# Products of the identity ahead of TensorE's waits, and the stores of x2 moved to SyncE, in a fused decoder layer

## The chip, the cores and the metric

The kernel runs on one NeuronCore of one Trainium2 chip. The metric is the device time of one execution in microseconds (us). The engines are TensorE (PE, with its weight loads as PEld), VectorE (DVE), ScalarE (ACT), GpSimd (POOL) and SyncE (SP, which only issues transfers).

## The reference

One layer over x of shape (32, 256, 256), all in float32, cut to what matters:

```python
x = layernorm(x + mamba(x, ...))               # conv, silu, softplus, scan over 16 states
x = layernorm(x + cross_attention(x, ctx))     # 16 heads of 16, 256 queries x 256 keys
x = layernorm(x + expert_ffn(x))               # 8 experts, D_FF = 704; tokens split by position
```

In cross_attention each head makes `scores = q @ k.T / sqrt(16)`, a softmax, and `attn @ v`; the 16 heads are joined and multiplied by `w_o`. In expert_ffn expert e works on positions 32e to 32e+31 of every one of the 32 batches (`h = silu(x @ w1[e]) * (x @ w3[e]); out = h @ w2[e]`), so the experts start when the last batch has left the second layernorm.

## The kernel before, in words

There are two programs, one after the other on the same core: `mixers` (mamba and attention, batch by batch) and `experts`. Within `mixers` every engine has its own list of steps. `run_steps` (its code stands below) sorts them by a number: a step with offset o runs for batch b at position 16*b + o, and steps at one position in the order of the list. So up to six batches are in flight at once, and one engine works in strict program order: a step that waits holds up all that stands behind it.

**The attention of a batch.** The queries and keys are split into high and low parts, stored to DRAM (`store_parts`), and loaded back stacked by SP (`load_stack(gr)`, lines 430 and 432: nine transfers for four heads; it waits until the previous batch's `scores_T` has read these heads). PE makes `scores(hd)` (tile s_ps, or dA_ps0 at the end), DVE takes the row maximum (`row_max`, L863), PE transposes the maxima of four heads (`max_transpose`, L1100), ACT and DVE split them (L716, L869), and ACT stores and reloads them as two more rows of q_st (L726, L735: max_rows_dram). Then PE makes the scores again, transposed (`scores_T`, tile st_ps or dA_ps1), ACT takes the exponential (L679, probs), and PE multiplies by v (`pv(gr)`, f_ps<-probs,v). ACT evacuates (L690, oT), PE transposes back (`head_transpose(gr)`, L1143), DVE normalises (L883, L888, tile on). PE transposes `on` (L1060), ACT evacuates (L696), PE makes `attn_out` (a_ps<-w_o,x1T), DVE adds the residual and takes moments (L838 to L847), ACT normalises (L631 to L642, `norm(1, ...)`), which completes x2 of the batch in x_tok. It is then stored to DRAM as rows (`store_x2`, L671, four transfers, x_rows<-x_tok, issued by ACT), and transposed by PE (L1060, a_ps<-ident,x_tok), evacuated by ACT (L705; of the last batch first its first columns, L703) and stored as columns (`store_x2T`, L463, issued by SP).

**The drain.** After the scans of batch 31 (POOL has then nothing more to do, and DVE only its part of the attention) PE, ACT and DVE finish the attention of batches 29, 30 and 31. Meanwhile SP loads weights of the first expert (L184, L190), then, in `load_tokens` and `load_columns`, the tokens of the first expert. `load_columns` waits for the stored columns of batch 30 (L175, 96 KB). At the end of `mixers` all engines meet (L200) and `experts` begins on PE with `gate_up` (L1376: g_ps and u_ps), which waits for these columns.

**Precision.** The operands of the scores are float32r (rounded), read in one record per product; a product of ordinary float32 operands shows as two MATMUL records in the trace, and a PE transpose as one. The count x8 on a row of the trace with float32 operands is thus four products.

PE's transposes and products share three PSUM banks (`bank_a`, `bank_f`, `bank_y`), and `wait_read` waits until a bank's last content has been read.

Of the kernel before, what the change touches and what calls it, by code (L numbers as in the profile page):

```python
# [14 lines left out]
P = 128  # L15
B, L, D = 32, 256, 256
# [5 lines left out]
TT = L // P  # L22
H, DK = 16, 16
HG = 4
NG = H // HG
# [5 lines left out]
EC = L // E  # L31
# [17 lines left out]
NX = 4  # L49
# [26 lines left out]
O_ONT = 78  # L76
O_OF = 80
O_N2 = 82
# [117 lines left out]
def mixers(nc, io, x2_dram, scratch, shared):  # L196
# [3 lines left out]
    with ExitStack() as ctx:  # L200
# [144 lines left out]
        def _(sp):  # L345
# [112 lines left out]

            def store_x2T(b):

                dst = shared.x2T_dram.rearrange("k e p t -> p (k e) t")[:, :, EC * b.c:EC * (b.c + 1)]
                wait_all(sp, (s_x2T, 1, b, 1))
                sp.dma_start(dst, x2T[:].rearrange("p k (e t) -> p (k e) t", t=EC)).then_inc(s_x2T_st, 16)  # L463
# [16 lines left out]
                *[(O_LD + HG * gr - 2, load_stack(gr)) for gr in range(NG)],  # L480
                (O_X2T + 3, load_columns),
# [58 lines left out]
        def _(act):  # L540
# [124 lines left out]
            def store_x2(b):  # L665

                rows = x2_dram.rearrange("(a e n r) d -> n e r a d", a=TT, e=P // EC, r=EC)
                rows = rows[bass.ds(b.c, 1)].rearrange("n e r a d -> (n e) r a d")
                wait_all(act, (s_x2, TT, b, TT))
                for q in range(X2_DMAS):  # L670
                    act.dma_start(rows[q], xt[EC * q:EC * (q + 1), b.c % NX]).then_inc(s_x2_st[b.par], 16)  # L671

# [57 lines left out]
            def max_load(gr):  # L730
# [14 lines left out]
                (O_N2 + 3, store_x2),  # L745
# [170 lines left out]
        def _(pe):  # L916
# [8 lines left out]

            pe.wait_ge(s_zero, 1)
# [121 lines left out]

            def x_of(b):
                return xt[:, b.c % NX]  # L1050
# [28 lines left out]
            def scores(hd):  # L1079

                def piece(b):
                    pe.wait_ge(s_stack[hd // HG], b.value(STACK_DMAS * 16, STACK_DMAS * 16))
                    n = b.value(H, hd)
                    if n:
                        pe.wait_ge(s_max, n - 1 if n > LATE_S + 1 else n)
                    if n == LATE_S + 1:
                        pe.wait_ge(s_hC_v, len(HC_DVE) * B)
                        for half in range(2):
                            pe.wait_ge(s_scan[half], NU * B)
                    out = scores_bank(n)  # L1090
                    for tt in range(TT):
                        i = mm(out[:, tt], q_st[:, hd, tt * P:(tt + 1) * P], k_st[:, hd], True, True)
                    i.then_inc(s_s_mm, 1)
                return piece

            def max_transpose(gr):
                def piece(b):
                    pe.wait_ge(s_max, b.value(H, HG * gr + HG))
# [7 lines left out]
            def scores_T(hd):  # L1106

                def piece(b):
                    pe.wait_ge(s_m_row, b.value(NG * 16, 16 * (hd // HG) + 16))
# [7 lines left out]
                    out = scores_T_bank(n)  # L1117
                    for kt in range(TT):
                        i = mm(out[:, kt], k_st[:, hd, kt * P:(kt + 1) * P], q_st[:, hd], True, True)
# [3 lines left out]
            def pv(gr):  # L1123

                def piece(b):
                    pe.wait_ge(s_exp, b.value(H, HG * gr + HG))
# [11 lines left out]
            def head_transpose(gr):  # L1138
                def piece(b):
                    pe.wait_ge(s_oT, b.value(NG, gr + 1))  # L1140
# [8 lines left out]
            def attn_out(tt):  # L1149
                def piece(b):  # L1150
                    pe.wait_ge(s_onT, b.value(1, 1))
# [22 lines left out]
                *[(O_K, k_proj(m)) for m in range(KD)],  # L1174
                (O_ONT - 2, transpose(lambda b: on, s_on, NG, s_onT_mm, s_onT, bank_a, a_ps)),
                *[(O_Q, q_proj(m)) for m in range(KD)],
                (O_X2T, transpose(x_of, s_x2, TT, s_x2T_mm, s_x2T, bank_a, a_ps)),
                *[(O_ON + HG * gr, head_transpose(gr)) for gr in range(NG)],
# [318 lines left out]
```

## Time and profile before

| | |
|---|---|
| time, median of 3 runs | 2745.58 us (2741.46 to 2746.72) |
| the profiled execution | 2741.8 us; its span 2740.0 us |
| PE busy | 2429.5 us (89%) |
| DVE busy | 2123.5 us (77%) |
| ACT busy | 1821.1 us (66%) |
| POOL busy | 2073.6 us (76%) |
| mean granted TensorE clock | 0.952 |

The span runs from the first to the last instruction. Busy shares are means over the stages: POOL works in `mixers` only and is idle from about 2159 us on; `experts` starts at 2257.47 us and is work of PE without a gap nearly to the end. The granted clock is given as a share of 2.4 GHz: 1.00 is 2.4 GHz, 0.50 is 1.2 GHz, and numbers between are means over a stretch that has both.

### The profile page before, as it was taken

The numbers are of one execution on the slowest core, as the hardware profiler recorded it, in microseconds if no ns is written. First come the engines' busy times: TensorE is split into PE (matmuls) and PEld (weight loads), VectorE is DVE, ScalarE is ACT, GpSimd is POOL, SyncE is SP. The second block draws the span as 40 slices with busy tenths as digits, with TensorE's granted clock in tenths as the row PEclk, the third lists the DMA queues.
The fourth block names the chain that finished last, engine by engine and source line by source line (L and its number), as shares of the span: only waits on it lengthen the run. The fifth ranks groups of instructions, "written<-read, shape, count | busy, mean of one in ns | idle before, by whom it ended". The sixth has DMA issues, their size and how long they took to land. (4 is left out here: it accounts for less than half of the span.)

```text
span 2740.0 us, 49530 instructions
## 1 busy us (share of the span) xinstructions
PE 2429.5 (89%) x14854; PEld 1667.0 (61%) x14854; DVE 2123.5 (77%) x3232; ACT 1821.1 (66%) x3972; POOL 2073.6 (76%) x999
## 2 busy tenths in 40 slices
PE   6678898989898898889999989988997879999997
PEld 5456666666666666666666666666665545555554
DVE  3788999999999999999999999999999722222333
ACT  3667888888888888888888887888887531111111
POOL 5999999999999999999999999999999400000000
PEclk9888999999999999999999999999998869999999
DMA  5355666666666666666666666666665342432221
GB/s 154 112 152 147 168 168 161 160 167 170 175 161 168 171 171 163 163 165 167 165 165 176 160 177 162 171 163 160 160 160 156 101 118 65 119 120 80 80 80 31
DMA packets 270168, 399.66 MB, mean 146 GB/s; under 512 B 115441, under 2 KB 190449, under 8 KB 265810
## 3 DMA queue, kind: packets, MB, share of 16 engines
q1 hardware_dynamic: 254546, 384.95, 52.9%
q10 hardware_dynamic: 15360, 11.55, 1.6%
q8 instruction: 124, 2.03, 0.3%
q14 instruction: 138, 1.13, 0.2%
HBM read 300.89 MB, written 94.37 MB: 144 GB/s over the span
## 5 line engine op out<-in xcount | busy, mean ns | idle before, releaser
L519 POOL TENSOR_TENSOR arena<-arena 128x1024 f32<-128x1024 f32 x512 | 1207.6, 2364 | 33.6 <-DMA arena<-w_dram 33.3
L623 ACT ACTIVATE dA_ps<-arena,a_neg 128x256 f32<-128x256 f32 x2048 | 880.1, 465 | 256.3 <-DVE arena L800 125.7
L800 DVE TENSOR_TENSOR_SCAN arena<-dA_ps,arena 128x512 f32<-128x512 f32 x672 | 802.7, 1207 | 75.5 <-ACT dA_ps L623 52.2
L529 POOL TENSOR_TENSOR arena<-arena 128x1024 f32<-128x1024 f32 (+1 forms) x416 | 808.4, 1943 | 18.0 <-DVE arena L800 15.0
L800 DVE TENSOR_TENSOR_SCAN dA_ps<-dA_ps,arena 128x512 f32<-128x512 f32 x352 | 415.7, 1204 | 3.8 <-POOL arena L519 3.4
L920 PE MATMUL a_ps<-xT,w_conv 128*128 128x256 f32 x1536 | 367.3, 389 | 0.0
L863 DVE TENSOR_REDUCE mx<-s_ps 128x2 f32<-128x512 f32 x497 | 333.4, 671 | 18.6 <-PE s_ps L920 18.6
L920 PEld LDWEIGHTS a_ps<-xT,w_conv 128*128 128x128 f32 x1536 | 286.5, 193 | 53.9 <-issue 16.3
L679 ACT ACTIVATE probs<-st_ps 128x512 f32<-128x512 f32 x493 | 285.2, 578 | 27.6 <-PE st_ps L920 25.4
L920 PE MATMUL s_ps<-k_st,q_st 96*128 96x256 f32 x994 | 262.2, 346 | 38.8 <-DVE mx L863 29.3
L920 PE MATMUL y_ps<-arena,sel 128*32 128x256 f32 x4096 | 258.5, 395 | 37.5 <-POOL arena L529 33.9
L920 PE MATMUL st_ps<-q_st,k_st 96*128 96x256 f32 x986 | 220.3, 306 | 35.3 <-ACT probs L679 29.6
L813 DVE TENSOR_TENSOR arena<-dA_ps,arena 128x512 f32<-128x512 f32 x352 | 230.7, 676 | 4.4
L920 PEld LDWEIGHTS s_ps<-k_st,q_st 96*128 96x128 f32 x994 | 167.8, 197 | 85.6 <-issue 55.3
L920 PEld LDWEIGHTS st_ps<-q_st,k_st 96*128 96x128 f32 x986 | 156.0, 196 | 96.1 <-issue 85.1
L1305 DVE TENSOR_TENSOR hT<-silu,u_ps 128x512 f32<-128x512 f32 x80 | 54.9, 686 | 193.8 <-PE u_ps L1376 161.0
L920 PEld LDWEIGHTS y_ps<-arena,sel 128*32 128x32 f32 x4096 | 126.4, 113 | 128.0 <-POOL arena L529 34.1
L1278 ACT ACTIVATE silu<-g_ps 128x512 f32<-128x512 f32 (+1 forms) x96 | 56.4, 596 | 210.0 <-PE g_ps L1376 209.9
L1376 PE MATMUL g_ps<-arena 128*128 128x512 f32 x384 | 181.7, 599 | 2.7 <-PEq L200 2.7
L920 PE MATMUL a_ps<-bias 2*128 2x512 f32 (+2 forms) x192 | 93.0, 485 | 98.5 <-DVE parts L853 39.9
L920 PE MATMUL f_ps<-probs,v 128*32 128x256 f32 x2048 | 156.0, 428 | 0.8 <-ACT probs L679 0.7
L1376 PE MATMUL u_ps<-arena 128*128 128x512 f32 x320 | 150.5, 592 | 0.0
(117 smaller groups left out, 3275.4 us busy)
## 6 DMA issues: line engine op xcount, KB each, us to landing
arena<-delta_dram SPq DMA_DIRECT2D x512, 128.0 KB, 2.9
arena<-w_dram SPq DMA_DIRECT2D x512, 128.0 KB, 3.3
arena<-bc_dram SPq DMA_DIRECT2D x128, 256.0 KB, 4.5
q_st<-q_parts_dram SPq DMA_DIRECT2D x512, 64.0 KB
k_st<-k_parts_dram SPq DMA_DIRECT2D x512, 64.0 KB
w_dram<-u SPq DMA_DIRECT2D x32, 512.0 KB, 3.1
delta_dram<-delta SPq DMA_DIRECT2D x32, 512.0 KB, 3.9
k_parts_dram<-parts SPq DMA_DIRECT2D x32, 512.0 KB, 4.2
```

What stands on the lines that cost most here:

```text
L519: pool.tensor_tensor(dBu[:, n % NB], w_r[:, n // RP % 2, t % RP].unsqueeze(1).to_broadcast([P, QS, L]), bc_r[:, b.par, 0], ALU.mult).then_ ...
L529: pool.tensor_tensor(h[:, n % NH, states], h[:, n % NH, states], bc_r[:, b.par, 1, states], ALU.mult).then_inc(s_hC, 1)
L623: last = nc.scalar.activation(dA[n % NDA][:, q], delta_r[:, n // (2 * RP) % 2, t % RP], ACT.Exp, scale=a_neg[:, t, 2 * half + q:2 * half + ...
L679: nc.scalar.activation(probs[:, n % NPROB], scores_T_bank(n), ACT.Exp, scale=float(DK) ** -0.5).then_inc(s_exp, 1)
L800: nc.vector.tensor_tensor_scan(dst, decays, dBu[:, n % NB, 2 * half:2 * half + 2].rearrange("p q t -> p (q t)"), 0.0, ALU.mult, ALU.add).t ...
L813: nc.vector.tensor_tensor(h[:, n % NH, 2 * half:2 * half + 2], state[:], bc_r[:, b.par, 1, 2 * half:2 * half + 2], ALU.mult).then_inc(s_hC ...
L863: nc.vector.tensor_reduce(mx[:, hd], scores_bank(b.value(H, hd)), AX.X, ALU.max).then_inc(s_max, 1)
L920: return nc.tensor.matmul(out, lhsT, rhs, start=first, stop=last)
L1278: nc.scalar.activation(dst, g_ps[i % 2][first:last], ACT.Silu).then_inc(f_silu, 1)
L1305: nc.vector.tensor_tensor(hT[first:last, i // 2, HALF * (i % 2):HALF * (i % 2 + 1)], silu[first:last, i % 2], ups[first:last], ALU.mult).t ...
L1376: ins = nc.tensor.matmul(ps[i % 2][:], w13[:, b.par, k, col:col + P], x2T[:, b.par, k, cols], start=(k == 0), stop=(k == KD - 1))
```

## The change

Two things change. First, PE is given products of the identity with itself (`drain_products`, 128x128 float32, into a bank that nobody reads then) in front of the waits of the last batch: 11 before the scores of head 0, 4 before each of the first two transposes of maxima, 6, 6 and 12 before the transposed scores of heads 4, 8 and 12, 5 before `pv` of the last two groups, 4, 22, 4 and 5 before the four `head_transpose`, 4 before the transposes of `on`, 5 before `attn_out`, 34 before the transposes of x2 and 16 behind them; and 11 before the second `head_transpose` of batch 30. These are 158 products. In `scores` and `scores_T` the wait for the loaded rows moves behind them. Second, `store_x2` goes from ACT's list (offset O_N2 + 3) to SP's (O_N2 + 4), for all 32 batches.

```diff
@@ -456,6 +456,14 @@
+            def store_x2(b):
+
+                rows = x2_dram.rearrange("(a e n r) d -> n e r a d", a=TT, e=P // EC, r=EC)
+                rows = rows[bass.ds(b.c, 1)].rearrange("n e r a d -> (n e) r a d")
+                wait_all(sp, (s_x2, TT, b, TT))
+                for q in range(X2_DMAS):
+                    sp.dma_start(rows[q], xt[EC * q:EC * (q + 1), b.c % NX]).then_inc(s_x2_st[b.par], 16)
+
@@ -478,6 +486,7 @@
                 *[(O_LD + HG * gr - 2, load_stack(gr)) for gr in range(NG)],
+                (O_N2 + 4, store_x2),
                 (O_X2T + 3, load_columns),
                 (O_X2T + 3, store_x2T),
@@ -662,14 +671,6 @@
-            def store_x2(b):
...
@@ -742,7 +743,6 @@
-                (O_N2 + 3, store_x2),
@@ -923,6 +923,15 @@
+            def drain_products(b, count, out=None):
+                if b.c < B - 1:
+                    return
+                if out is None:
+                    bank_y.wait_read(pe)
+                    out = y_ps[:, 0:P]
+                for _ in range(count):
+                    mm(out, ident[:], ident[:], True, True)
+
@@ -1046,6 +1055,11 @@
+            def idle(count):
+                def piece(b):
+                    drain_products(b, count)
+                return piece
+
@@ -1079,7 +1093,6 @@
             def scores(hd):
                 def piece(b):
-                    pe.wait_ge(s_stack[hd // HG], b.value(STACK_DMAS * 16, STACK_DMAS * 16))
...
                     out = scores_bank(n)
+                    drain_products(b, {0: 11}.get(hd, 0), out[:, 0, 0:P])
+                    pe.wait_ge(s_stack[hd // HG], b.value(STACK_DMAS * 16, STACK_DMAS * 16))
@@ -1095,6 +1110,7 @@
             def max_transpose(gr):
                 def piece(b):
+                    drain_products(b, 4 if gr < 2 else 0)
                     pe.wait_ge(s_max, b.value(H, HG * gr + HG))
@@ -1106,7 +1122,6 @@
             def scores_T(hd):
-                    pe.wait_ge(s_m_row, b.value(NG * 16, 16 * (hd // HG) + 16))
...
                     out = scores_T_bank(n)
+                    drain_products(b, {4: 6, 8: 6, 12: 12}.get(hd, 0), out[:, 0, 0:P])
+                    pe.wait_ge(s_m_row, b.value(NG * 16, 16 * (hd // HG) + 16))
@@ -1123,6 +1140,7 @@
             def pv(gr):
+                    drain_products(b, 5 if gr >= NG - 2 else 0)
@@ -1137,6 +1155,9 @@
             def head_transpose(gr):
+                    drain_products(b, (4, 22, 4, 5)[gr])
+                    if gr == 1 and b.c == B - 2:
+                        drain_products(b.ahead(1), 11)
@@ -1148,6 +1169,7 @@
             def attn_out(tt):
+                    drain_products(b, 5 if tt == 0 else 0)
@@ -1172,9 +1194,12 @@
+                (O_ONT - 2, idle(4)),
                 (O_ONT - 2, transpose(lambda b: on, s_on, NG, s_onT_mm, s_onT, bank_a, a_ps)),
                 *[(O_Q, q_proj(m)) for m in range(KD)],
+                (O_X2T, idle(34)),
                 (O_X2T, transpose(x_of, s_x2, TT, s_x2T_mm, s_x2T, bank_a, a_ps)),
+                (O_X2T, idle(16)),
```

On PE, at the end of `mixers` (from the last `head_transpose` of batch 31 on, then the first products of `experts`), before:

```order
L1143 MATMUL f_ps<-ident,oT 128x128 x2
L1060 MATMUL a_ps<-ident,on 128x128 x4
L1060 MATMUL a_ps<-ident,x_tok 128x128 x4
L920 MATMUL a_ps<-bias 128x512
L920 MATMUL a_ps<-w_o,x1T 128x256 x4
L1060 MATMUL a_ps<-ident,x_tok 128x128 x4
L200 UNCONDITIONAL_BRANCH
L1354 UNCONDITIONAL_BRANCH
L1376 MATMUL g_ps<-arena 128x512 x2
```

And in the changed kernel, the same place (line numbers have moved: 1143 is 1164, 1060 is 1074, 1376 is 1401):

```order
L1164 MATMUL f_ps<-ident,oT 128x128 x2
L920 MATMUL y_ps<-ident 128x128 x4
L1074 MATMUL a_ps<-ident,on 128x128 x4
L1074 MATMUL a_ps<-ident,x_tok 128x128 x4
L920 MATMUL y_ps<-ident 128x128 x5
L920 MATMUL a_ps<-bias 128x512
L920 MATMUL a_ps<-w_o,x1T 128x256 x4
L920 MATMUL y_ps<-ident 128x128 x34
L1074 MATMUL a_ps<-ident,x_tok 128x128 x4
L920 MATMUL y_ps<-ident 128x128 x16
L200 UNCONDITIONAL_BRANCH
```

The order of the real products is the same; 59 identity products stand between them, 34 of them directly in front of the transposes of x2 and 16 in front of the meeting of the engines.

On PE, earlier in the drain (batch 31 alone: `scores_T` of heads 8 to 12, `pv(1)`, `head_transpose(1)`), in the changed kernel:

```order
L920 MATMUL st_ps<-ident 128x128 x6
L920 MATMUL st_ps<-q_st,k_st 128x256 x2
L920 MATMUL f_ps<-probs,v 32x256 x8
L920 MATMUL dA_ps1<-q_st,k_st 128x256 x2
L920 MATMUL st_ps<-q_st,k_st 128x256 x2
L920 MATMUL y_ps<-ident 128x128 x22
L1164 MATMUL f_ps<-ident,oT 128x128 x2
L920 MATMUL dA_ps1<-q_st,k_st 128x256 x2
L920 MATMUL st_ps<-ident 128x128 x12
L920 MATMUL st_ps<-q_st,k_st 128x256 x2
```

Before, the same rows stand there without the three that read only `ident`.

On SP, the end of `mixers`, from the weights of the first expert to the columns of batch 31, before:

```order
L184 DMA arena<-in_w 128x2x704
L463 DMA x_columns<-x2T_batch 128x16x32
L175 DMA arena<-x_columns 128x2x896
L170 DMA arena<-x_rows 128x7x256
L463 DMA x_columns<-x2T_batch 128x16x32
L175 DMA arena<-x_columns 128x2x96
L463 DMA x_columns<-x2T_batch 128x16x32
```

And in the changed kernel:

```order
L465 DMA x_rows<-x_tok 32x2x256 x4
L184 DMA arena<-in_w 128x2x704
L471 DMA x_columns<-x2T_batch 128x16x32
L465 DMA x_rows<-x_tok 32x2x256 x4
L175 DMA arena<-x_columns 128x2x896
L170 DMA arena<-x_rows 128x7x256
L471 DMA x_columns<-x2T_batch 128x16x32
L465 DMA x_rows<-x_tok 32x2x256 x4
L175 DMA arena<-x_columns 128x2x96
L471 DMA x_columns<-x2T_batch 128x16x32
```

The three rows of L465 are the stores of batches 29, 30 and 31. That of 29 stands behind `load_stack(2)` and ahead of `load_stack(3)` of batch 31 (not shown), that of 30 ahead of the tokens of the first expert, and that of 31 ahead of the 96 KB of columns on which `gate_up` waits.

## Rows read from the trace of the kernel before

**Rows 1.** The page: 40 slices of the span, and one of the costliest groups.

```profile
POOL 5999999999999999999999999999999400000000
PEclk9888999999999999999999999999998869999999
...
L519 POOL TENSOR_TENSOR arena<-arena 128x1024 f32<-128x1024 f32 x512 | 1207.6, 2364 | 33.6 <-DMA arena<-w_dram 33.3
```

**Rows 2.** Windows of the drain: stretch, its length, busy (records) by engine, PEclk.

```profile
2200.50:2214.40 13.90, 13.53 (x74) 10.12 (x75) 6.79 (x14) 5.95 (x12) 0.00 (x0) 0.50 0.49 138
2229.20:2257.50 28.30, 16.22 (x70) 9.21 (x70) 3.24 (x13) 8.53 (x20) 0.00 (x0) 0.52 0.17 38
```

**Rows 3.** Timeline of PE in the drain: start, length, work, count [idle before].

```profile
2194.36 0.51 PE L920 MATMUL s_ps<-k_st,q_st 96*128 96x256 f32 x2 [1.59 <-DMA q_st<-k_st]
...
2198.84 0.41 PE L1143 MATMUL f_ps<-ident,oT 128*128 128x128 f32 x2 [1.58 <-ACT oT L690]
...
2207.39 0.77 PE L920 MATMUL s_ps<-k_st,q_st 96*128 96x256 f32 x2
...
2214.49 0.78 PE L920 MATMUL s_ps<-k_st,q_st 96*128 96x256 f32 x2
...
2229.19 0.41 PE L1143 MATMUL f_ps<-ident,oT 128*128 128x128 f32 x2 [3.07 <-ACT oT L690]
...
2231.77 0.80 PE L920 MATMUL st_ps<-q_st,k_st 96*128 96x256 f32 x2 [1.63 <-DMA q_st<-max_rows_dram]
...
2245.66 3.78 PE L920 MATMUL a_ps<-w_o,x1T 128*128 128x256 f32 x8
2253.69 1.12 PE L1060 MATMUL a_ps<-ident,x_tok 128*128 128x128 f32 x4 [4.25 <-ACT x_tok L642]
2257.47 3.75 PE L1376 MATMUL g_ps<-arena 128*128 128x512 f32 x4 [2.67 <-PEq L200]
```

**Rows 4.** Timeline of PE, the spacing of small products at the full clock.

```profile
2155.73 1.99 PE L920 MATMUL a_ps<-w_o,x1T 128*128 128x256 f32 x8
...
2179.70 0.40 PE L920 MATMUL s_ps<-k_st,q_st 96*128 96x256 f32 x2
2179.94 0.40 PE L920 MATMUL st_ps<-q_st,k_st 96*128 96x256 f32 x2
...
2188.55 0.60 PE L1060 MATMUL a_ps<-ident,x_tok 128*128 128x128 f32 x4
```

**Rows 5.** The same timeline at the very start of the kernel.

```profile
1.18 9.04 PE L920 MATMUL s_ps<-g 128*128 128x256 f32 x32 [1.18 <-DVE g L765]
```

**Rows 6.** The chain that ended last, a later group of gate_up.

```profile
2262.99 1.72 PE g_ps L1376 x4
```

**Rows 7.** Timeline of all engines, the end of batch 31.

```profile
2248.06 0.36 SPq L175 DMA_DIRECT2D arena<-x_columns  x1
...
2252.56 1.08 ACT L642 ACTIVATE x_tok<-x_tok,shift,rstd 128x256 f32<-128x256 f32 x2
2253.66 1.76 ACTq L671 DMA_DIRECT2D x_rows<-x_tok  x4
```

**Rows 8.** Timeline of SP, the stacked loads of batch 31.

```profile
2192.00 0.59 SPq L432 DMA_DIRECT2D q_st<-k_st  x1
...
2199.88 0.30 SPq L430 DMA_DIRECT2D q_st<-q_parts_dram  x1
...
2203.52 0.59 SPq L432 DMA_DIRECT2D q_st<-k_st  x1
```

**Rows 9.** Timeline of SP and ACT in a batch of the steady stage.

```profile
1238.95 1.08 ACT L642 ACTIVATE x_tok<-x_tok,shift,rstd 128x256 f32<-128x256 f32 x2
...
1252.27 0.60 SPq L432 DMA_DIRECT2D q_st<-k_st  x1
...
1261.77 1.71 SPq L395 DMA_DIRECT2D arena<-delta_dram  x4
```

**Rows 10.** DMA issues near the end of mixers: size, median us to landing.

```profile
arena<-x_columns SPq DMA_DIRECT2D x1, 96.0 KB, 2.4
```

More of the change, by code:

```diff
@@ L663, in bc_store @@
                 act.dma_start(bc_dram[b.par], xp[RANK:RANK + 2 * NS]).then_inc(s_bc_st, 16)
-            def store_x2(b):
[L667 to L671, printed above, removed]
             def softmax_exp(hd):
```

## The prediction

> **What bounds the kernel now.** I read the page first. POOL shows 9 in nearly every slice of `mixers`, so up to about 2159 us the elementwise products of the scan set the pace; its one large wait is for a load of w, 33.3 us in all [rows 1]. From 2257.47 us on the last chain is PE without a break: the experts [rows 3, 6]. Between lies the drain, some 100 us, in which PE is busy but hands over to ACT, DVE and transfers again and again. The PEclk line has its one 6 there [rows 1]. The windows show why: 0.50, the lower level of 1.2 GHz, from 2200.50 to 2214.40, and 0.52 from 2229.20 to the end of `mixers` [rows 2]. What the engine did before each fall stands in its timeline: it had waited 1.59 and 1.58 us shortly before 2200, and 3.07 us just before 2229.19 [rows 3]. The price of the low clock is seen best on equal work: the eight records of `attn_out` take 1.99 us at 2155.73 [rows 4] and 3.78 us at 2245.66 [rows 3]; the first four of `gate_up` take 3.75 us [rows 3], the same form later 1.72 [rows 6].
>
> So there is something to win. What is at stake is the start of `gate_up`, 2257.47, and the pace of its first records; behind it nothing changes.
>
> **What a product costs.** This is the number on which all hangs, and the trace has no float32 product of 128 columns. An ordinary float32 product is two records; with 256 columns, eight records take 1.99 us, about 0.21 each after the first. The stream of 128 columns would be half of that, 0.107 a record, 0.213 us a product. But each record also loads 128 weight columns. The nearest rows with loads of that width and a stream of 0.107 us are the scores (two records of 256 float32r columns): pairs start at 2179.70 and 2179.94, so 0.24 us for two records [rows 4]. I take 0.24 us a product at the full clock, with 0.213 as the near bound. The far bound is the transpose, also 128x128 float32 but one record: four in 0.60 us, (0.60 - 0.27)/3 = 0.11 us each, where 0.27 is the tail of the last one [rows 4]. At the low clock all of these double, as `attn_out` does. 158 products are 38 us of PE at 0.24 (34 at 0.213, 17 at 0.11).
>
> The waits of PE that they are put into are shorter than that. 11 products are 2.64 us for a wait of 1.59; the other 11 stand in one of 1.58; 22 are 5.3 us for 3.07; 12 are 2.9 for 1.63; 34 are 8.2 for 4.25; 16 are 3.8 for 2.67 [rows 3]. At 0.11 each run fits its wait (1.2, 1.2, 2.4, 1.3, 3.7, 1.8). The wait of 4.25 is the clearest: it is the residual, moments and layernorm on DVE and ACT, from the end of `attn_out` at 2249.44 to the end of L642 at 2253.64 [rows 3, 7], and no clock of PE shortens or lengthens it.
>
> The Trainium skill (FP8 and Floating Point Precision, section TensorE Precision Notes) says that a true float32 product takes four passes through the array. That agrees with the records of 256 columns above (1.99 us for four products, less the tail, is near 4 x 256 columns at 2.4 GHz each), and by it alone a product of 128 columns is 0.213 us, the near bound; the sum would then be the -2.4 us below.
>
> **The drain replayed.** I walk through PE's order with 0.24 us for a product, the full clock for everything, and the measured durations for what ACT, DVE and the transfers do.
> - Scores of head 0 of batch 31: 11 products from 2192.6, so 2195.3, not 2194.36. The second run of 11 starts at 2198.2 and ends at 2200.85, where `head_transpose` had started at 2198.84: 2.0 us late.
> - The scores of heads 8 to 11 come 6.1 us after the `scores_T` that frees their rows: 4.2 us in which SP issues nine transfers (2199.88 to 2204.11) and 1.8 us of landing (the last issue of the first stack ends at 2192.59, its reader starts at 2194.36) [rows 3, 8]. That `scores_T` ends at 2201.8 in the replay, 2.0 us late, so the reader starts at 2207.9, against 2207.4 before: there it did not wait for its load, and the low clock had used up the slack.
> - Between the stacks of heads 8 to 11 and 12 to 15 SP now issues the four stores of batch 29, 1.8 us [rows 7], so the last stack is issued at 2208.0 to 2212.2 and read at 2214.0. It was read at 2214.5 [rows 3]: SP's own store eats what the clock would give here.
> - From there the scores, `pv` and the transposes run at the full clock, but 6 + 4 + 6 products (3.8 us) go in: `scores_T` of head 8 at 2223.5. Then 22 products: `head_transpose(1)` at 2230.4 (2229.19 before), 1.2 us late. Then 12: `scores_T` of head 12 at 2233.8 (2231.77), 2.0 us late.
> - 5, 4, 5 and 5 more, each in a wait of some 0.6 us, against half the time for 16 records of `pv` twice: the last `head_transpose` at 2241.3. The transposes and `attn_out`, at the full clock and with 4 and 5 products, end at 2247.5 against 2249.44: 1.9 us early.
> - 34 products: the transposes of x2 start at 2255.6 instead of 2253.69, although x2 is ready at 2251.7. 16 products and 0.7 us for the engines to meet: `gate_up` at 2260.6, 3.1 us late.
> - `gate_up` then starts at the full clock: 3.75 becomes 1.72, -2.0 us [rows 3, 6].
>
> Sum: +3.1 - 2.0 = +1.1 us. The same walk at 0.213 us puts the same places at 2195.0, 2207.4, 2213.5, 2229.1, 2232.2, 2245.4, 2252.5 and 2257.1: -0.4 - 2.0 = -2.4 us. I forecast the middle of these two, -0.7 us. At most places the ends of the two walks differ by less than the counts suggest, because part of each run still lies in a wait.
>
> **The stores on SP.** In the steady stage each batch adds four issues, 1.8 us, to SP, behind a stacked load and ahead of the next load of delta. SP idles there from 1252.87 to 1261.77, 8.9 us [rows 9], waiting for its turn with that buffer; x2 is ready 12 us before, at 1240.03, so the stores neither wait nor delay the load. If the cover were gone it would be 1.8 us for each of 32 batches, 58 us, but some 7 us of it remain. ACT loses 1.8 us of issue a batch, which it did beside its activations; POOL is the bound [rows 1], so I put this at nothing. At the very end it frees ACT: L703 waited until the issue at 2253.66 was over, 1.76 us long [rows 7], about 0.7 us behind the transposes. That is hidden behind PE's 16 products. In its place `load_columns` moves behind the four stores of batch 31: 96 KB that were asked for at 2248.06 are now asked for 1.8 us after the layernorm and land 0.4 + 2.4 us later [rows 7, 10], 4.6 us after it: 2256.3 in my replay, hidden as long as the products hold PE to 2260. If PE were earlier, this becomes the wait that starts the experts.
>
> **Rivals.**
> - *A product costs what a transpose does (0.11 us).* For it: same shape, same operand. Against it: no ordinary float32 product in the trace shows as one record. The overruns vanish; the replay then has 2212.0 for head 12 (-2.5, SP's stack), 2224.3 for `head_transpose(1)` (-4.9), 2226.0 for head 12 transposed (-5.8), the end of `attn_out` at 2237.4 (-12.0), x2 ready at 2241.6, and `gate_up` at 2246.2, held by the 96 KB: -11.3 - 2.0 = -13.3 us, 2732.3 us.
> - *The low clock stays, slower than before.* The windows say that the scores and `pv` alone do not raise it: PE was busy 13.53 of 13.90 us at 0.50 [rows 2]. At the start of the kernel 32 records in 9.04 us, where 32 x 0.213 are 6.8, say that some 10 dense records ran at half speed first [rows 5]. If the clock falls at about 2205 again, where only 4 products stand in 7 us, then 6 + 4 + 6 + the first 9 of the 22 run at 0.48: 25 x 0.24 = +6.0 us, and what the clock gave between is gone as well: +1.1 + 6.0 + 1 = +8 us, 2753.7 us. This decides from about 20 products at the low clock on.
> - *The stores held on SP delay a load in the steady stage.* Only where SP's idle time of 8.9 us shrinks under 1.8; no batch that I looked at does. Its price from one such batch in four would be 8 x 1.8 = 14 us.
>
> **How the numbers follow.** The replay with its two prices, 0.5; the cheap product, 0.3, since it alone makes every run of products fit its wait; the low clock, 0.15; the stores, 0.05. The profiled execution before took 2741.8 us, 3.8 under the median of 2745.58; I add the difference of -0.7 to the median: 2744.9. The likeliest case alone holds 2741 to 2749 (prices of 0.213 to 0.26, and some microseconds of the runs' own spread, 2741.46 to 2746.72). For eight in ten the range goes to the cheap product below, 2732, and most of the way to the low clock above, 2751. A measurement of this kernel can tell 0.2%, 5.5 us. Faster by more: the cheap product, and a little of the replay's low side, 0.33. Slower by more: low clock, stores, 0.17. Within: 0.5.
>
> **What would show it.** In the profile after: the mean spacing of the 34 products (8.2 us in all; 7.3 or 3.7 by the bounds); a transposition of x2 that starts at once behind them while x2 has been ready for 3 us or more; PEclk near 1.00 from 2192 to 2262, with 2205 to 2214 as the doubtful part; `gate_up` in 1.72 us from its first group; SP's stores between the last two stacked loads. A product at 0.11 us makes the forecast wrong, and then `gate_up` should wait for the 96 KB of columns.

## The result, and the profile after

The changed kernel takes 2750.52 us (median of 20 runs, 2744.6 to 2756.96), the kernel before, run beside it, 2743.14 us (20 runs, 2737.86 to 2747.37). The ratio is 1.0025, interval 1.0016 to 1.0034: some 7 us slower. The forecast was no change, with -0.7 us. The execution whose profile is shown took 2745.45 us, 5.1 us under its kernel's median, so the profiled pair shows only part of the loss.

The page after, against [rows 1]; 40 slices, then two of the costliest groups (L528 is L519 of before, L538 was L529):

```profile
POOL 5999999999999999999999999999999400000000
PEclk8798999999999999999999999999998899999999
...
L528 POOL TENSOR_TENSOR arena<-arena 128x1024 f32<-128x1024 f32 x512 | 1209.9, 2369 | 27.3 <-DMA arena<-w_dram 26.8
L538 POOL TENSOR_TENSOR arena<-arena 128x1024 f32<-128x1024 f32 (+1 forms) x416 | 811.0, 1950 | 26.3 <-DVE arena L800 24.0
```

The 6 in PEclk is gone, so the products did what they are there for. But POOL's second group now waits 26.3 us. Its first group waits less than in [rows 1], 27.3 us against 33.6, so the two together wait 53.6 us against 51.6. The second group's row of before:

```profile
L529 POOL TENSOR_TENSOR arena<-arena 128x1024 f32<-128x1024 f32 (+1 forms) x416 | 808.4, 1943 | 18.0 <-DVE arena L800 15.0
```

The windows of the drain answer to [rows 2], moved by 2.0 us at the first and 4.1 to 5.4 us at the second:

```profile
2202.50:2216.40 13.90, 11.59 (x101) 8.84 (x101) 7.43 (x17) 7.22 (x16) 0.00 (x0) 1.00 0.42 109
2233.30:2262.90 29.60, 28.42 (x252) 26.04 (x250) 3.25 (x13) 7.72 (x18) 0.00 (x0) 1.00 0.34 92
```

The clock is 1.00 where it was 0.50 and 0.52. The timeline of PE answers to [rows 3]:

```profile
2194.89 0.27 PE L1116 MATMUL y_ps<-ident,mx 128*8 128x128 f32 x1
2194.99 2.62 PE L920 MATMUL s_ps<-ident 128*128 128x128 f32 x22
2197.37 0.48 PE L920 MATMUL s_ps<-k_st,q_st 96*128 96x256 f32 x2
...
2209.57 0.47 PE L920 MATMUL s_ps<-k_st,q_st 96*128 96x256 f32 x2 [0.50 <-DMA q_st<-k_st]
...
2216.19 0.47 PE L920 MATMUL s_ps<-k_st,q_st 96*128 96x256 f32 x2 [1.33 <-DMA q_st<-k_st]
...
2228.46 5.08 PE L920 MATMUL y_ps<-ident 128*128 128x128 f32 x44
2233.38 0.38 PE L1164 MATMUL f_ps<-ident,oT 128*128 128x128 f32 x2
...
2248.90 1.99 PE L920 MATMUL a_ps<-w_o,x1T 128*128 128x256 f32 x8
2250.73 7.75 PE L920 MATMUL y_ps<-ident 128*128 128x128 f32 x68
2258.32 0.60 PE L1074 MATMUL a_ps<-ident,x_tok 128*128 128x128 f32 x4
2258.76 3.74 PE L920 MATMUL y_ps<-ident 128*128 128x128 f32 x32
2262.95 1.95 PE L1401 MATMUL g_ps<-arena 128*128 128x512 f32 x4 [0.45 <-PEq L200]
```

x68 are the records of 34 products. Less the tail of the last one, a product is (7.75 - 0.27)/34 = 0.220 us, between the forecast's two prices. x2 was ready at 2255.09 (end of L651, once L642), and its transposes begin 3.2 us later, when the products are through; with half the products (an experiment below) they follow x2 in 0.5 us.

### Two stretches in which the time is counted

I measure every kernel below in the same two stretches.

- *Steady stage*: from the second MEMSET of delta on POOL to the 32nd; there is one a batch.
- *Drain*: from the transposition of maxima directly ahead of the scores of head 0 of batch 31 to the end of the first group of `gate_up`. (That transposition is the last of batch 30; some expectations below call it `max_transpose(1)` of batch 31, and mean the same row.)

The first two marks, on POOL's timeline, before:

```profile
92.59 0.13 POOL L510 MEMSET delta<- 128x16 f32 x1
2074.10 0.12 POOL L510 MEMSET delta<- 128x16 f32 x1
```

and after:

```profile
92.57 0.13 POOL L519 MEMSET delta<- 128x16 f32 x1
2077.35 0.13 POOL L519 MEMSET delta<- 128x16 f32 x1
```

So the steady stage is 1981.5 us before and 1984.8 after, +3.3. The drain is 68.7 before (2192.50 to 2257.47 + 3.75) and 70.0 after (2194.89 to 2262.95 + 1.95): +1.3, close to the forecast's +1.1. The forecast's sum for the drain held; most of what was measured lies where it expected nothing. One profile of each can't carry that alone, so the experiments had to.

Between the two stretches lie another 118.4 us before and 117.5 after. Over all profiles below this piece is 118.5 us in the mean with the old order of two waits and 117.8 with the new one (single values 115.8 to 120.4), so it doesn't hide a loss.

### The profile page after: what moved, and what is told of

It is laid out like the page before. It is cut to its first block and busy times, and to the rows that moved or that the text cites. A ratio compares the mean times of both kernels' runs of the same rounds, so it can differ in the third digit from the quotient of the medians.

```text
span 2743.6 us, 50161 instructions
## 1 busy us (share of the span) xinstructions
PE 2453.4 (89%) x15170; PEld 1692.6 (62%) x15170; DVE 2122.6 (77%) x3232; ACT 1821.7 (66%) x3972; POOL 2074.9 (76%) x999
## 5 line engine op out<-in xcount | busy, mean ns | idle before, releaser
L528 POOL TENSOR_TENSOR arena<-arena 128x1024 f32<-128x1024 f32 x512 | 1209.9, 2369 | 27.3 <-DMA arena<-w_dram 26.8
L800 DVE TENSOR_TENSOR_SCAN arena<-dA_ps,arena 128x512 f32<-128x512 f32 x672 | 802.4, 1207 | 70.8 <-ACT dA_ps L632 52.4
L538 POOL TENSOR_TENSOR arena<-arena 128x1024 f32<-128x1024 f32 (+1 forms) x416 | 811.0, 1950 | 26.3 <-DVE arena L800 24.0
L800 DVE TENSOR_TENSOR_SCAN dA_ps<-dA_ps,arena 128x512 f32<-128x512 f32 x352 | 415.7, 1204 | 5.3 <-POOL arena L528 3.4
L920 PE MATMUL y_ps<-arena,sel 128*32 128x256 f32 x4096 | 258.8, 395 | 36.4 <-POOL arena L538 34.5
```

What stands on the lines that cost most here:

```text
L528: pool.tensor_tensor(dBu[:, n % NB], w_r[:, n // RP % 2, t % RP].unsqueeze(1).to_broadcast([P, QS, L]), bc_r[:, b.par, 0], ALU.mult).then_ ...
L538: pool.tensor_tensor(h[:, n % NH, states], h[:, n % NH, states], bc_r[:, b.par, 1, states], ALU.mult).then_inc(s_hC, 1)
L800: nc.vector.tensor_tensor_scan(dst, decays, dBu[:, n % NB, 2 * half:2 * half + 2].rearrange("p q t -> p (q t)"), 0.0, ALU.mult, ALU.add).t ...
L920: return nc.tensor.matmul(out, lhsT, rhs, start=first, stop=last)
```

## The experiments

All medians are of 5 to 12 runs of the variant against 29 to 35 of before. First the four that take the change apart.

**Stores alone.** No products; the stores on SyncE and the moved waits stay.

```diff
 def drain_products(b, count, out=None):
-    if b.c < B - 1:
-        return
+    return
```

> Stores of x2 on SyncE, no identity product at all. Theory A (the whole loss is the products that overrun their waits): within 2 us of the kernel before, at most +1 us since the 96 KB of columns are now asked for behind the four stores. Theory B (the products cost only some 1 to 4 us as in the profiled pair, and the stores on SyncE cost the rest in the steady stage): +4 to +6 us over the kernel before.

Measured: 2743.12 us, ratio 1.0008 (0.9994 to 1.0021), some 2 us, between the two theories and too near to both for the interval to tell. The drain is 65.2 us, 3.5 less than before, which neither theory had.

**Products alone.** `store_x2`, with ScalarE as the issuer again, is back in its list.

```diff
-                (O_N2 + 4, store_x2),          # SyncE
+                (O_N2 + 3, store_x2),          # ScalarE
```

> All 158 products, stores of x2 on ScalarE as before. Theory A: +6 to +8 us over the kernel before, as the changed kernel. Theory B: +1 to +2 us.

Measured: 2754.18 us, ratio 1.0040 (1.0026 to 1.0054), the slowest of all: 11 us over before, more than either theory had (+6 to +8, +1 to +2). Its drain is 74.5 us. Windows of it, with the clock ahead of the last two columns:

```profile
2205.00:2216.00 11.00, 9.68 (x86) 8.29 (x84) 5.91 (x13) 6.19 (x16) 0.00 (x0) 1.00 0.47 126
2216.00:2226.00 10.00, 8.36 (x51) 6.61 (x51) 3.67 (x9) 3.52 (x7) 0.00 (x0) 0.66 0.79 244
```

and its timeline of PE there:

```profile
2216.92 0.77 PE L920 MATMUL st_ps<-q_st,k_st 96*128 96x256 f32 x2 [1.52 <-DMA q_st<-max_rows_dram]
...
2226.91 0.50 PE L920 MATMUL st_ps<-q_st,k_st 96*128 96x256 f32 x2 [1.63 <-DMA q_st<-max_rows_dram]
```

Here the clock falls once more: it is 0.50 from 2217 to 2223, behind a wait for the rows of maxima, which ScalarE stores and reloads. Less the 7.1 us by which this drain began later than before's, that is 2210 to 2216, in and just behind the stretch that the rival of the low clock called doubtful (2205 to 2214). This kernel differs from the changed one only in who issues the stores, so with them on ScalarE the products did not hold the clock; the evidence is one profile of each.

**Half of every count** (76 products), and **half of the last two runs only** (34 to 17, 16 to 8).

```diff
-                (O_X2T, idle(34)),
+                (O_X2T, idle(17)),
...
-                (O_X2T, idle(16)),
+                (O_X2T, idle(8)),
```

> Both parts of the change, but about half of every count of products (76 in place of 158: 17 and 8 at the end), so that at 0.226 us a product each run fits its wait. Theory A: the overruns vanish and the clock stays high, gate_up starts 11 us or more before that of the changed kernel, so some 5 us under the kernel before. Theory B: the same gain in the drain, less 5 us lost in the steady stage, so also 11 us under the changed kernel. If the clock falls in the drain instead, it is no faster than the kernel before.

> The change with only the last two runs halved, 17 and 8 in place of 34 and 16. Both theories: the transposes of x2 start when x2 is ready, 3.2 us earlier, and gate_up then waits for the 96 KB of columns, so 3 to 3.5 us under the changed kernel.

Measured: half of all 2739.93 us, 0.9991 (0.9980 to 1.0003), drain 61.5; half of the tail 2744.47 us, 1.0008 (0.9996 to 1.0020), drain 67.9. The last transposes now follow x2 within 0.5 us. The clock of the kernel with half of all is 1.00 from 2192 to 2254. It does not last to the end: `gate_up` waits for the 96 KB and then starts at the low clock, 3.68 us for its first group where the changed kernel has 1.95:

```profile
2257.84 3.68 PE L1401 MATMUL g_ps<-arena 128*128 128x512 f32 x4 [1.94 <-DMA arena<-x_columns]
```

So too with half of the tail (3.36 us, behind a wait of 1.97). There `gate_up` starts 3.5 us earlier in the drain than in the changed kernel, as expected, and loses 1.4 of it again to the clock. Halving the tail thus takes 2.1 us off the drain, halving the rest another 6.4, so the runs of products ahead of the tail cost more than the tail. The gain in time of half of all, some 2 us, is what its theory B leaves, not the 5 us of theory A.

These four fell into a pattern: each took 3 to 6 us more than its drain gave. What they all share with the changed kernel, and not with before, is the order of two waits in all 32 batches.

**The waits alone; before once more; the whole change with the old order of the waits in batches 0 to 30.** The edit of the last:

```diff
 def scores(hd):
     def piece(b):
+        if b.c < B - 1:
+            pe.wait_ge(s_stack[hd // HG], ...)
...
         drain_products(b, {0: 11}.get(hd, 0), out[:, 0, 0:P])
-        pe.wait_ge(s_stack[hd // HG], ...)
+        if b.c == B - 1:
+            pe.wait_ge(s_stack[hd // HG], ...)
```

and the same in `scores_T` with s_m_row.

> No products, stores of x2 on ScalarE as before; of the change only this is left: in scores and scores_T the wait for the loaded rows stands behind the wait for the free bank, in all 32 batches. Before this run, the five changed kernels sit 3 to 6 us above what their profiled drains (from max_transpose(1) of batch 31 to the first group of gate_up) would give against the profiled execution of before. Theory A, the swapped waits cost something small in each batch: ratio 1.001 to 1.002, 3 to 6 us above before. Rival B, the offset comes from the one profiled execution of before, whose drain or start was not typical: ratio 1.000 within 0.0008. Rival C, it comes from the stores or the products: also 1.000 here.

> The kernel before, unchanged, as if it were a variant: ratio 1.000, its own interval shows what the comparison can tell. Its second profile is what is wanted. Rival B: max_transpose(1) of batch 31 lies 2 us or more after the 2192.5 us of the first profile, as in all five changed kernels (2194.2 to 2201.6), or the stretch from it to the first group of gate_up, the group included, is 3 us or more off the 68.7 us of the first profile. Theory A or C: it lies at 2192.5 within 1.5 us and the stretch is 68.7 within 1.5 us.

> The changed kernel with all its 158 products and the stores on SyncE, but in batches 0 to 30 the wait for the loaded rows stands ahead of the wait for the bank again, as before; only in batch 31 it stands behind the products. Theory A: the offset goes, ratio about 1.0005 (the +1.3 us of the drain alone), against 1.0025 of the changed kernel. Rivals B and C: as the changed kernel, 1.002 to 1.003.

Measured: the waits alone 2747.68 us, 1.0023 (1.0011 to 1.0035); before again 2744.03 us, 1.0004 (0.9993 to 1.0016), steady stage 1984.6, drain 68.4; the whole change with the old order 2741.51 us, 1.0001 (0.9992 to 1.0010). Two lines of code that look like tidying, and nothing else, cost as much as the whole change did, within the intervals. Taking them back takes the loss back, with all 158 products still in. That is theory A, a little above its 1.001 to 1.002. Of rival B one sign came true: in the second profile of before the first mark of the drain lies at 2198.36, 5.9 us later than in the first, whose `mixers` were thus on the short side. But the drain agrees (68.4 against 68.7), and before again takes the same time as before.

The waits of POOL between 250 and 2160 us (us in total, times, longest) tell the two orders apart. Before:

```profile
POOL arena L519 <- DMA arena<-w_dram: 17.4, 20, 2.2
POOL arena L529 <- DVE arena L800: 15.0, 21, 1.9
```

The changed kernel:

```profile
POOL arena L538 <- DVE arena L800: 23.3, 25, 1.9
POOL arena L528 <- DMA arena<-w_dram: 11.9, 16, 1.7
```

The whole change with the old order:

```profile
POOL arena L528 <- DMA arena<-w_dram: 22.3, 29, 1.8
POOL arena L538 <- DVE arena L800: 13.8, 19, 1.9
```

In the new order POOL, the bound of this stage, waits 8 to 10 us longer for VectorE's scans and 5 to 10 us less for its loads of w. In these three profiles the one nearly makes up for the other. The cost shows over all 17 profiles: POOL is busy for 1934.7 to 1936.3 us of the steady stage in each of them, and all its waits between 250 and 2160 us add up to 45 us in the mean with the old order in `scores_T` (42.9 to 47.0) and to 51 with the new one (45.9 to 54.8). The changed kernel's profile has the 45.9, the lowest of its group.

**Columns first.** With half of the products `gate_up` waited 1.94 us for the 96 KB. Here their load is issued ahead of the stores of batch 31.

```diff
+                (O_N2 + 4, load_columns),
                 (O_N2 + 4, store_x2),
-                (O_X2T + 3, load_columns),
```

> Half of the products at each place (76 in all), stores of x2 on SyncE, and the last load of columns (96 KB) is issued ahead of the four stores of batch 31. With half the products (ratio 0.9991) the first group of gate_up waited 1.94 us for these columns, behind the stores. If that wait is SyncE's order of issue, it goes, gate_up follows the transposes of x2 and the 8 products at once, and the time is 1.9 us lower: ratio 0.9984, the stretch from max_transpose(1) to the end of the first group 59.6 us against 61.5. Rival: the columns are late for another reason (the layernorm frees nothing earlier, or the landing of 2.4 us), then 61.5 stays and the ratio is 0.9991.

Measured: 2737.90 us, 0.9987 (0.9977 to 0.9997); the drain 58.6 us, 2.9 less than with half the products alone. The wait was SyncE's order of issue, and the rival falls. Only 1.2 us of the 2.9 are the earlier start; the other 1.7 are the first group, which runs at the full clock again (1.96 us against 3.68), and the expectation did not have that. Its timeline at the end:

```profile
2244.51 0.36 SPq L175 DMA_DIRECT2D arena<-x_columns  x1
2246.91 1.08 ACT L651 ACTIVATE x_tok<-x_tok,shift,rstd 128x256 f32<-128x256 f32 x2
2248.01 1.75 SPq L465 DMA_DIRECT2D x_rows<-x_tok  x4
2248.04 0.66 PE L1074 MATMUL a_ps<-ident,x_tok 128*128 128x128 f32 x4 [0.46 <-ACT x_tok L651]
...
2251.09 1.96 PE L1401 MATMUL g_ps<-arena 128*128 128x512 f32 x4 [0.60 <-PEq L200]
```

The columns are asked for 3.5 us ahead of the stores, and `gate_up` waits only for the meeting of the engines.

**All of it together, and the parts of the swap.** The version that the runs pointed to (half of the products, columns first, old order of the waits); the swap of the waits in `scores` alone and in `scores_T` alone, on the kernel before; and the stores on SyncE alone with the old order.

```diff
 def scores_T(hd):
     def piece(b):
-        pe.wait_ge(s_m_row, b.value(NG * 16, 16 * (hd // HG) + 16))
...
         out = scores_T_bank(n)
+        pe.wait_ge(s_m_row, b.value(NG * 16, 16 * (hd // HG) + 16))
```

> What the runs so far point to: half of the products (76), stores of x2 on SyncE, the last columns loaded ahead of the stores of batch 31, and in batches 0 to 30 the waits in the order of before. If the pieces add up, with the swapped waits that kernel is 0.9987, and the swap alone costs 0.0023: ratio 0.9965 to 0.997, 2733 to 2734 us, and GpSimd's last MEMSET of delta lies 1981 to 1985 us behind its second, as in the three profiles with the old order, not 1984.5 to 1992.5. Rival: the swap costs nothing once the stores are on SyncE, ratio 0.9987.

> The kernel before with the waits swapped in scores alone (stack behind bank), without products or other changes. The swap of both costs 1.0023 (5 to 6 us). If it is the first wait of scores that costs, the ratio is 1.002 and GpSimd waits 22 to 31 us for scans of VectorE between 250 and 2160 us (14 to 15 with the old order); if it is that of scores_T, 1.000 and 14 to 15 us.

> The kernel before with the waits swapped in scores_T alone (rows of maxima behind bank). If it is the wait of scores_T that costs, the ratio is 1.002 and GpSimd waits 22 to 31 us for VectorE; if that of scores, 1.000 and 14 to 15 us. If each gives half, 1.001 both times, the cost lies in many small shifts.

> Of the change only the stores of x2 on SyncE, for all 32 batches, the waits in the order of before in batches 0 to 30, no products. The same with swapped waits was 1.0008 with a drain (max_transpose(1) of batch 31 to the end of the first group of gate_up) of 65.2 us against 68.7. If the prediction was right that the stores cost nothing in the steady stage, only the drain is left: -3 us, ratio 0.9988. If they cost there, 1.000 or above.

Measured: all together 2733.75 us, 0.9966 (0.9949 to 0.9983), some 9 us faster than before, as expected (its steady stage, 1985.9 us, is 1 us outside the range given); `scores` swapped 2744.40, 1.0004 (0.9987 to 1.0020); `scores_T` swapped 2745.47, 1.0010 (0.9996 to 1.0024); stores alone with the old order 2736.86, 0.9977 (0.9962 to 0.9992), so they cost nothing in the steady stage. In time neither half of the swap stands apart from no change, and neither reached the 1.002 named for it. In the trace they differ: POOL waits 25.8 us for L800 with `scores_T` swapped, within the 22 to 31 named, and 18.6 with `scores` swapped, between the two ranges named. With the stores alone, `gate_up` shows the wait that the forecast named for the case that PE is early:

```profile
2252.53 1.75 SPq L465 DMA_DIRECT2D x_rows<-x_tok  x4
...
2254.32 0.44 SPq L175 DMA_DIRECT2D arena<-x_columns  x1
2256.97 3.78 PE L1406 MATMUL g_ps<-arena 128*128 128x512 f32 x4 [3.31 <-DMA arena<-x_columns]
```

**A second wait in `scores_T`, and the whole change with one of the two orders old.**

```diff
 # the kernel before, scores_T: the wait ahead stays
         out = scores_T_bank(n)
+        pe.wait_ge(s_m_row, b.value(NG * 16, 16 * (hd // HG) + 16))
```

> The kernel before with one more wait in scores_T: the rows of maxima are waited for ahead of the bank, as before, and once more behind it, where they have long arrived. If what costs is that a wait already met stands between the wait for ScalarE's exponential and the product (theory A in its narrow form), the traces of the swapped kernels come back: GpSimd waits 22 to 31 us for VectorE between 250 and 2160 us, ScalarE's evacuation of v waits 15 to 19 us, the ratio is about 1.001. Rival: what costs is that the wait for the rows is taken late, then 12 to 16 us and 25 to 30 us, and 1.000.

> The changed kernel, with the old order of the waits in scores_T alone (batches 0 to 30). The swap alone in scores_T left the marks in the trace, that in scores hardly. So most of the offset should go: ratio 1.0005 to 1.001 (the changed kernel 1.0025, with both old 1.0001). Rival: both matter, about 1.0013.

> The changed kernel, with the old order of the waits in scores alone (batches 0 to 30), scores_T swapped as in the change. If scores_T carries the cost, the ratio stays at 1.002 to 1.0025 and GpSimd waits 22 to 31 us for VectorE; if scores carries it, 1.0005.

Measured: the second wait 2746.15 us, 1.0012 (1.0002 to 1.0023), POOL waits 31.4 us for L800; the whole change with `scores_T` in the old order 2745.66, 1.0010 (0.9997 to 1.0023), 14.9 us; with `scores` in the old order 2748.44, 1.0021 (1.0010 to 1.0033), 24.7 us. The waits of POOL follow `scores_T`. The times point the same way, as both expectations had it, though these two intervals overlap.

What the second wait tells depends on where the waits stand in the program as built. A product carries one wait itself, and others stand in a semaphore instruction ahead of it. The order of the built program, before:

```
L920 MATMUL st_ps<-q_st,k_st 128x256 [waits probs_ready,max_rows_loaded]
```

and, the same with `scores_T` swapped, with the second wait and in the changed kernel:

```
L920 MATMUL st_ps<-q_st,k_st 128x256 [waits max_rows_loaded,probs_ready]
```

```profile
L1112 PEldq EVENT_SEMAPHORE  x510: 51/51/51, 213.5 to 2235.8; - x170
L1117 PEldq EVENT_SEMAPHORE  x511: 51/51/51, 213.3 to 2241.4; - x171
L1118 PEldq EVENT_SEMAPHORE  x512: 51/51/2599, 209.3 to 2248.4; - x171
```

L1112 is the wait for the exponential, L1117 that for the rows of maxima. So the wait written first stays on the product (on its weight load, in the trace), and the one written later goes ahead of it. Before, the product carries the wait for the rows, and the wait for the exponential stands ahead of it. With `scores_T` swapped, and in the changed kernel, it is the other way round: the move behind the bank in the source is a move ahead in the built program. With the second wait (L1118) the extra instruction waits for both, and the product once more for the rows. That is a third form and no repetition of the swap.

All three forms differ in how soon PE starts when the exponential ends its wait. From the end of the exponential to the product it is 0.145 us before (28 places of the trace, 0.144 to 0.146), 0.053 with the swap and in the changed kernel (23 places each, 0.052 to 0.053), and 0.10 with the second wait (25 places, 0.098 to 0.100). Both quicker forms have the longer waits of POOL for L800 (25.8 and 31.4 us, against 15.0), and the ratios 1.0010 and 1.0012. ScalarE's wait for the product of v, of which the expectation speaks, divides the profiles too: 25.8 to 29.6 us in the seven with the old order in `scores_T`, 14.8 to 18.7 in the ten others, 17.1 with the second wait. So the marks that the expectation named for its theory came. The theory itself falls all the same: it blames a wait already met that stands between the wait for the exponential and the product, and that is just what before has, without the marks, and what the swapped kernels do not have.

The Trainium skill (Perfetto Trace Analysis, section Identifying Dependency Chains) says that an instruction which waits on several engines may get an extra semaphore instruction ahead of it for the rest. The traces agree: some 510 such instructions for the 512 heads of `scores_T` (16 in each of 32 batches). Which of the two waits stays on the product is decided by the order in the source.

### All variants in one table

Expected sum: 5.4 us where `scores_T` waits in the new order, plus the drain less 68.5 (the mean of the six without products and with the stores on ScalarE). Measured is (ratio - 1) x 2743; the intervals of these ratios are 2.5 to 4.7 us to either side.

| kernel | POOL <- L800 | steady stage | drain | sum | measured |
|---|---|---|---|---|---|
| before; again | 15.0; 13.9 | 1981.5; 1984.6 | 68.7; 68.4 | 0 | 0; +1.1 |
| `scores` swapped | 18.6 | 1983.0 | 70.1 | +1.6 | +1.1 |
| `scores_T` swapped; second wait | 25.8; 31.4 | 1985.4; 1993.6 | 68.3; 68.0 | +5.2; +4.9 | +2.7; +3.3 |
| both swapped | 30.8 | 1989.5 | 67.7 | +4.6 | +6.3 |
| stores, old order | 12.2 | 1981.4 | 65.1 | -3.4 | -6.3 |
| stores, new order | 28.7 | 1984.6 | 65.2 | +2.1 | +2.2 |
| products, new order | 25.5 | 1991.2 | 74.5 | +11.4 | +11.0 |
| **the change** | 23.3 | 1984.8 | 70.0 | +6.9 | +6.9 |
| the change, old order | 13.8 | 1982.0 | 69.9 | +1.4 | +0.3 |
| the change, `scores_T` old; `scores` old | 14.9; 24.7 | 1983.3; 1987.7 | 70.3; 69.9 | +1.8; +6.8 | +2.7; +5.8 |
| half tail | 28.2 | 1992.5 | 67.9 | +4.8 | +2.2 |
| half of all | 22.7 | 1991.1 | 61.5 | -1.6 | -2.5 |
| half, columns first | 28.3 | 1984.7 | 58.6 | -4.5 | -3.6 |
| half, columns first, old order | 14.3 | 1985.9 | 58.7 | -9.8 | -9.3 |

The seven profiles with the old order in `scores_T` have a steady stage of 1983.1 us in the mean (1981.4 to 1985.9), the ten with the new one 1988.5 (1984.6 to 1993.6); this is where 5.4 comes from. The second wait counts with the new order. The sums miss the measured by up to 2.9 us, so the table shows that the parts fit together, and not what each is worth to a microsecond. A single profile wanders by several microseconds there, so that no single pair would have shown it; the waits of POOL separate the two groups without overlap (12.2 to 18.6 and 22.7 to 31.4).

## Why the prediction was wrong

- **The step that failed is one that it did not take.** In the part on the change it costs the products, the clock and the stores, but puts no price on the moved waits in `scores` and `scores_T`, though the text on the change names them and they act in all 32 batches. They are worth some 6 us (1.0023 alone, 6.3 us; 1.0025 against 1.0001 in the whole change, 6.6 us). It looked for the change in the drain only, because there the products are. The text on the change has these waits move behind the products; in batches 0 to 30 there are no products, and in the built program the wait for the rows moves ahead of the other, as shown above.
- **The price of a product** was right: 0.220 us, between 0.213 and 0.24. The rival of 0.11 us, with a chance of 0.3, falls: a record takes 0.11, and a product has two, as the text's own argument against it had it.
- **The replay of the drain.** Moved by the 2.4 us by which its first mark was late, the changed kernel has the scores of head 8 at 2207.2 (forecast 2207.9 at 0.24 us), head 12 at 2213.8 (2214.0), `head_transpose(1)` at 2231.0 (2230.4), the end of `attn_out` at 2248.5 (2247.5), the transposes of x2 at 2255.9 (2255.6) and `gate_up` at 2260.6 (2260.6). All within 1 us, but in part by luck. At the measured 0.220 us, a quarter of the way from the low price to the high one, the same walk has 2229.4, 2245.9, 2253.3 and 2258.0 for the last four. So other terms between head 12 and the end of `attn_out` were some 2.5 us too small, and the price of 0.24 made up for them. Which terms these are is not shown.
- **The clock**: as forecast 1.00 throughout, and the first group of `gate_up` takes 1.95 us in place of 3.75. That is -1.8 us, not -2.0: the 1.72 of the forecast was read from the chain [rows 6], which counts a group only up to the next, and 3.75 from the timeline.
- **The stores on SyncE: half right.** In the steady stage they cost nothing (1981.4 us with them, old order). In the drain the forecast put them at nothing too, save that SyncE loads the last stack behind one of them, and that was mis-sized: the drain is 65.1 and 65.2 us with the stores on SyncE and no products, 68.5 with them on ScalarE, so moving them gives 3.4 us. The last reload of maxima, which ScalarE issues, leaves 37.7 and 37.3 us after the first mark in the two profiles of before, 36.4 and 34.8 with the stores moved, 34.0 in the changed kernel and 39.7 with products and the stores on ScalarE. That fits; the steps by which it becomes 3.4 us are not shown. The products then cost +4.9 us on top (65.1 to 70.0). The forecast's +1.1 for the two together came out right as a sum (+1.3), though it had no price for either part by itself.
- **The rival of the low clock** did not happen in the changed kernel, and did with the products alone. One of its premises is not shown: in the trace of before the granted clock is 1.00 in all of the first 12 us, where it read half speed from the spacing of the records [rows 5].
- **What stays open.** How the order of two waits lengthens the steady stage. Where PE is released by ScalarE's exponential, the new order even lets it start sooner. Before, ACT and PE at one of the 28 places:

```profile
1281.31 0.58 ACT L679 ACTIVATE probs<-st_ps 128x512 f32<-128x512 f32 x1
...
1282.03 0.47 PE L920 MATMUL st_ps<-q_st,k_st 96*128 96x256 f32 x2 [1.15 <-ACT probs L679]
```

and with both waits swapped:

```profile
1288.63 0.57 ACT L679 ACTIVATE probs<-st_ps 128x512 f32<-128x512 f32 x1
...
1289.26 0.50 PE L920 MATMUL st_ps<-q_st,k_st 96*128 96x256 f32 x2 [1.06 <-ACT probs L679]
```

From the end of the exponential to the product it is 0.14 us before (1281.89 to 1282.03) and 0.05 with the waits swapped. That the new order goes with longer waits of POOL for VectorE is shown by the totals; the path between is not shown by any run here, nor that it is this earlier start that does it.

## What to carry to other kernels

Read a diff for what it does in every iteration before what it does in the place it is about: here two reordered waits, which act 1024 times, outweighed 158 added products that act once. And read the order of waits in the built program, since it can be the reverse of the source's. Products that only keep the clock up must fit into the wait they stand in: half of them kept it up as well until `gate_up` waited for its columns, and took 8.5 us off the drain. When two effects of opposite sign are costed at nothing and at little, a right sum proves neither; only runs of each part alone do.

## What the runs showed of the hardware

- The order in which two waits of one product are written is not neutral. The wait written first stays on the product, the later one goes into an instruction ahead of it. The product starts 0.053 us after its releaser when it carries the wait that comes last itself (23 places of the changed kernel), and 0.145 us when that wait stands in the instruction ahead (28 places of before).
- A float32 product of 128x128 by 128 columns costs 0.220 us at the full clock in a dense run (34 in 7.75 us, less a tail of 0.27), two records of 0.11 us each.
- A wait of PE of 1.52 us was followed by a stretch at the lower clock (0.66 over 10 us, 0.50 from 2217 to 2223) although dense products stood ahead of it; in the changed kernel waits of 0.50 and 1.33 us in the same part of the drain left it at 1.00. The length of the wait alone does not decide: a wait of 1.63 us later in the same run, and one of 1.64 with half of all products, left it at 1.00 as well.
